# A two-layer block on one core: the rank-8 condition weights are generated between the steps of the first recurrence

## The reference, cut to what matters

```python
# first recurrence (L0_cond2), 512 steps
a = xw_t + prev_h @ Wh                     # xW = x @ Wx + b, 4*256 columns
i, f, o = sigmoid(a[:, :H]), sigmoid(a[:, H:2*H]), sigmoid(a[:, 2*H:3*H])
g = tanh(a[:, 3*H:])
next_c = f * prev_c + i * g;  next_h = o * tanh(next_c)
...
# condition of layer 1 (L1_cond), RANK = 8, D = 256, 8 rows of ada_emb
c = (ada_emb - mu) / sqrt(var + 1e-5) * ln_gamma + ln_beta
h = gelu(c @ W1 + bias1)
w = h @ W2 + bias2                         # W2: 256 x 4*256*8
a1, b1, a2, b2 = [t.reshape(B, D, R) for t in split(w, 4)]
u = x @ a2;  mid = gelu(x @ base_down + u @ b2.T)
out = mid @ base_up.T + (mid @ b1) @ a1.T;  x + out
```

## Time and profile before

| | us |
|---|---|
| median of 3 runs | 4209.75 |
| the profiled execution | 4171.73 |
| its span, first to last instruction | 4170.0 |
| PE busy (matmul) | 3372.0 (81%) |
| weight loads busy | 2464.0 (59%) |
| DVE busy | 2302.2 (55%) |
| ScalarE busy | 1551.2 (37%) |
| POOL busy | 1201.6 (29%) |
| mean granted clock of TensorE | 0.743 |

### The profile page before, as it was taken

One profiled execution on the slowest core, in us unless ns is written; L12 is line 12 of the kernel. 1 busy time (PEld: TensorE's weight loads), 2 busy tenths in 40 slices (PEclk: granted clock), 3 DMA queues, 4 the chain that ended last, 5 costly groups with the idle time before them and its releaser, 6 DMA issues. The chain is left out here.

```text
span 4170.0 us, 141505 instructions
## 1 busy us (share of the span) xinstructions
PE 3372.0 (81%) x57076; PEld 2464.0 (59%) x57076; DVE 2302.2 (55%) x6841; ACT 1551.2 (37%) x5111; POOL 1201.6 (29%) x1588
## 2 busy tenths in 40 slices
PE   6665638888888888479989399999999998999772
PEld 4443317777777777435563156666666657777562
DVE  4449844444444444368801577778877775555333
ACT  0112213333333333257700355556555553444331
POOL 0001260100000000033300064555555555444442
PEclk9789965555555555589959699999999995555686
DMA  4001000000000000111000100000000001110245
GB/s 118 4 30 35 25 20 3 3 3 3 3 3 3 3 3 3 53 49 26 15 29 0 46 2 2 2 2 2 2 2 2 2 12 52 34 33 30 79 119 165
DMA packets 106990, 106.95 MB, mean 26 GB/s; under 512 B 52669, under 2 KB 94086, under 8 KB 105899
## 3 DMA queue, kind: packets, MB, share of 16 engines
q1 hardware_dynamic: 98714, 78.68, 6.7%
q0 software_dynamic: 7824, 21.46, 1.4%
HBM read 71.10 MB, written 29.00 MB: 24 GB/s over the span
## 5 line engine op out<-in xcount | busy, mean ns | idle before, releaser
L638 PE MATMUL banks<-hp,whp 128*128 128x8 f16 x24576 | 741.1, 168 | 153.9 <-DVE hp L695 153.9
L638 PEld LDWEIGHTS banks<-hp,whp 128*128 128x128 f16 x24576 | 697.0, 104 | 235.1 <-DVE hp L695 234.3
L690 DVE SCALAR_TENSOR_TENSOR carry<-ig 128x16 f32<-128x16 f32 x512 | 93.1, 182 | 426.2 <-ACT ig L661 426.2
L661 ACT ACTIVATE ig<-banks 128x32 f32<-128x32 f32 x512 | 100.9, 197 | 610.0 <-PE banks L638 610.0
L1015 ACT ACTIVATE att_PH<-att_stp 128x1024 f16<-128x1024 f32 (+3 forms) x258 | 183.2, 710 | 374.5 <-PE att_stp L833 374.4
L1642 PE MATMUL rnn_banks<-rnn_hp,rnn_whp 128*128 128x8 f16 x6144 | 285.0, 171 | 30.8 <-ACT rnn_hp L1700 9.9
L1642 PEld LDWEIGHTS rnn_banks<-rnn_hp,rnn_whp 128*128 128x128 f16 x6144 | 251.1, 108 | 97.9 <-ACT rnn_hp L1700 69.4
L616 POOL COPY HT<-hist 128x128 f32 x64 | 21.2, 407 | 986.7 <-DVE hp L700 986.7
L1080 POOL TENSOR_TENSOR att_QK<-att_rot,att_QK 128x512 f16<-128x512 f32 x133 | 173.8, 1307 | 338.5 <-ACT att_QK L1007 338.5
L624 PE MATMUL banks<-xs,wxp 128*128 128x64 f16 x3168 | 264.1, 241 | 0.0
L951 DVE TENSOR_TENSOR att_PL<-att_P,att_PH 128x1024 f16<-128x1024 f32 (+3 forms) x257 | 234.0, 930 | 17.3 <-ACT att_P L1021 16.4
(11 more groups left out here) (555 smaller groups left out, 7831.0 us busy)
## 6 DMA issues: line engine op xcount, KB each, us to landing
exp_xt<-expert_rows_scratch SPq DMA_DIRECT2D x80, 129.0 KB, 2.3
edge_cb<-cols_scratch SPq DMA_DIRECT2D x16, 512.0 KB, 3.7
XT<-expert_found_scratch SPq DMA_DIRECT2D x16, 512.0 KB, 4.9
gen_w<-in_L_cond_W_dram SPq DMA_DIRECT2D x2, 3072.0 KB
mod_xn<-in_x_dram SPq DMA_DIRECT2D x8, 512.0 KB
XT<-in_xT_dram SPq DMA_DIRECT2D x1, 4096.0 KB
out_dram<-exp_ob SPq DMA_DIRECT2D x64, 64.0 KB, 2.2
attw_st<-in_L_attn_w_qkvT_dram SPq DMA_DIRECT2D x6, 512.0 KB
```

Source lines behind the costliest of these rows:

```text
L638: last=nc.tensor.matmul(out, whp[:,wpart,k,col:col+128], hp[:,k,hpart], start=False,stop=True,skip_group_check=True)
```

## The change

`load_lstm_weights` is replaced by `prepare_stage`, which brings the recurrence's weights and all small operands of the condition weights (15 transfers), and runs the layer norm, the hidden product and its Gelu; the hidden vector hT stays in SBUF. In `lstm_stage` SP brings W2 in 8 pieces of 128 x 8 columns, each twice (for the even iteration shifted by four places, for the odd one not), into one buffer, when PE has finished with the last piece. PE makes one product behind the projection in every other step of the second half of each iteration, 8 an iteration, 128 in all; at the 17th step it waits for the piece. Behind the loop stand the additions of the bias, the transposes and the copy. ScalarE makes the high parts of wx and wh instead of DVE, and PE's first projections wait for less. The prefetch in `ffn0_stage` and the first block of `cond1_stage` are gone; the setup of constants on POOL moves into `prepare_stage`.

```diff
-def lstm_stage(nc, XT, HT, wx, wh, bias, h0T, T=T):
+def lstm_stage(nc, XT, HT, wx, wh, bias, h0T, g, W2, ident, T=T):
...
+        @block.sync
+        def _(sp):
+            with loop(nc,sp,NIT) as it:
+                sp.wait_ge(generated,it+1)
+                sp.sem_inc(sp_passed,1)
+                for k in range(2):
+                    piece=W2[k*P:(k+1)*P,:].rearrange("p (a n) -> p a n",n=PIECE)[:,bass.ds((it>>1).with_bounds(min_val=0,max_val=7),1),:].rearrange("p a n -> p (a n)")
+                    sp.dma_start(w2[:,k,bass.ds(RANK//2-(it&1)*(RANK//2),PIECE)],piece).then_inc(w2_in,16)
...
             pe.wait_ge(init,2)
-            pe.wait_ge(wsplit,7)
-            pe.wait_ge(h0split,4)
+            pe.wait_ge(w_hi,1)
+            pe.wait_ge(wsplit,4)
             pe.wait_ge(x_staged,2)
+            pe.sem_inc(generated,1)
+            def generate(it,m):
+                r_,k=divmod(m,2)
+                w=w2[:,k,RANK//2:RANK//2+PIECE].rearrange("p (d r) -> p r d",r=RANK)[:,r_]
+                return nc.tensor.matmul(ps_w[:,bass.ds((it*(RANK//2)+r_)*NB,NB)],w,hT[:,k],start=(k==0),stop=(k==1),skip_group_check=True)
             for half in range(2):
                 for tile in TILES: last=project(0,half,*tile)
             last.then_inc(x_projected,1)
+            pe.wait_ge(w_hi,2)
+            pe.wait_ge(wsplit,5)
+            pe.wait_ge(h0split,4)
...
+                    if s==C: pe.wait_ge(w2_in,it*32+32)
                     pe.wait_ge(hi_ready, it*2*C+s)
...
+                    if st==1 and cs%2==1: last=generate(it,cs//2)
+                    if s==2*C-1: last.then_inc(generated,1)
+            pe.wait_ge(biased,8)
+            for j,q in enumerate((0,3)):
+                for o in range(2): i=nc.tensor.transpose(ps_r[0:BR,j*D+o*P:j*D+(o+1)*P],wT[:,q,o,:],ident[:,:])
+            i.then_inc(rows,1)
         @block.scalar
         def _(act):
+            nc.scalar.activation(wxp[:,0],wx[:,:,:],ACT.Copy).then_inc(w_hi,1)
+            nc.scalar.activation(whp[:,0],wh[:,:,:],ACT.Copy).then_inc(w_hi,1)
...
-            for n,(src,dst) in enumerate(((wx,wxp),(wh,whp))):
-                nc.vector.tensor_copy(dst[:,0],src[:,:,:]).then_inc(wsplit,1)
-                dve.wait_ge(wsplit,2*n+1)
-                nc.vector.tensor_tensor(dst[:,1],src[:,:,:],dst[:,0],ALU.subtract).then_inc(wsplit,1)
+            dve.wait_ge(w_hi,1)
+            nc.vector.tensor_tensor(wxp[:,1],wx[:,:,:],wxp[:,0],ALU.subtract).then_inc(wsplit,1)
...
+            dve.wait_ge(w_hi,2)
+            nc.vector.tensor_tensor(whp[:,1],wh[:,:,:],whp[:,0],ALU.subtract).then_inc(wsplit,1)
...
+            dve.wait_ge(generated,NIT+1)
+            for q in range(4):
+                for k in range(2):
+                    at=(q*2+k)*BR
+                    nc.vector.tensor_tensor(wT[:,q,k,:].rearrange("p (b r) -> p b r",r=RANK),ps_w[:,at:at+BR].rearrange("p (r b) -> p b r",b=NB),b2[:,q,k:k+1,:].broadcast_to([P,NB,RANK]),ALU.add).then_inc(biased,1)
+            dve.wait_ge(rows,1)
+            nc.vector.tensor_copy(wR[:,:,:],ps_r[0:BR,:].rearrange("p (q d) -> p q d",q=2))
...
-                for dst,src in prefetch: sp.dma_start(dst,src).then_inc(prefetched,16)
...
-def load_lstm_weights(nc, wx, wh, bias, Wx, Wh, b):
+def prepare_stage(nc, wx, wh, bias, g, early, ident):
...
+            for n,(to,given) in enumerate(early): sp.dma_start(to,given).then_inc(early_in if n<5 else weights_in,16)
...
+            dve.wait_ge(early_in,80)
+            X_=mybir.AxisListType.X
+            step(nc.vector.tensor_reduce(out=st[:,0:1],in_=c[:,:],axis=X_,op=ALU.add))
...
+            for k in range(2): step(nc.vector.tensor_scalar(cT[:,k],ps_c[:,k*NB:(k+1)*NB],ga[:,k:k+1],be[:,k:k+1],ALU.mult,ALU.add))
+            dve.wait_ge(weights_in,160)
             for w in (wx[:,:,3*NH:4*NH],wh[:,:,3*NH:4*NH],bias[:,3*NH:4*NH]): nc.vector.tensor_scalar(w,w,2.0,None,ALU.mult).then_inc(doubled,1)
             dve.wait_ge(doubled,3)
...
+            for o in range(2):
+                for k in range(2): i=nc.tensor.matmul(ps_h[:,o*NB:(o+1)*NB],w1[:,k,o*P:(o+1)*P],cT[:,k],start=(k==0),stop=(k==1))
+            i.then_inc(hid,1)
```

More of the change, by code:

```diff
@@ L587, in lstm_stage @@
         NIT=T//(2*C); HALF=C//2
+        PIECE=P*RANK; w2=sb("gen_w2",[P,2,PIECE+RANK]); BR=NB*RANK
+        ps_w=ctx.enter_context(nc.psum_tensor("gen_ps_w",[P,512],F32)); ps_r=ctx.enter_context(nc.psum_tensor("gen_ps_r",[P,512],F32))
+        hT,b2,wT,wR=[g[n] for n in ("hT","b2","wT","wR")]
+        w2_in=sem("w2_in"); generated=sem("generated"); sp_passed=sem("sp_passed"); biased=sem("biased"); rows=sem("rows"); w_hi=sem("w_hi")
         block=ctx.enter_context(nc.Block())
@@ L1390, in cond1_stage @@
+        up,down,mask,wT,wR,nw,eps,ones=[g[n] for n in "up,down,mask,wT,wR,nw,eps,ones".split(",")]
         u=sb("u",[BR,T]); v=sb("v",[BR,T]); mid=sb("mid",[P,2,T]); sq=sb("sq",[P,2,2,T]); rs=sb("rs",[P,2,T]); rr=sb("rr",[P,2,T])
@@ new lines, in _ @@
+        @block.gpsimd
+        def _(pool):
+            nc.gpsimd.memset(ones[:,:],1.0).then_inc(const,1)
+            nc.gpsimd.memset(eps[:,:],float(np.finfo(np.float32).eps)).then_inc(const,1)
+            nc.gpsimd.memset(st[:,4:5],1e-5).then_inc(const,1)
+            nc.gpsimd.memset(mask[:,:],1.0).then_inc(const,1)
+            pool.wait_ge(const,4)
+            nc.gpsimd.affine_select(out=mask[:,:],in_=mask[:,:],compare_op=ALU.is_ge,fill=0.0,base=0,pattern=[[-RANK,NB]],channel_multiplier=1).then_inc(const,1)
+            pool.wait_ge(const,5)
+            nc.gpsimd.affine_select(out=mask[:,:],in_=mask[:,:],compare_op=ALU.is_ge,fill=0.0,base=RANK-1,pattern=[[RANK,NB]],channel_multiplier=-1).then_inc(const,1)
+            pool.wait_ge(const,6)
@@ L2023, in _ @@
+            dve.wait_ge(weights_in,160)
             for w in (wx[:,:,3*NH:4*NH],wh[:,:,3*NH:4*NH],bias[:,3*NH:4*NH]): nc.vector.tensor_scalar(w,w,2.0,None,ALU.mult).then_inc(doubled,1)
             dve.wait_ge(doubled,3)
+        @block.scalar
+        def _(act):
+            act.wait_ge(dv,5); act.wait_ge(const,3)
+            nc.scalar.activation(st[:,2:3],st[:,1:2],ACT.Sqrt,scale=1.0/D,bias=st[:,4:5]).then_inc(root,1)
+            act.wait_ge(hid,1)
+            for k in range(2): i=nc.scalar.activation(hT[:,k],ps_h[:,k*NB:(k+1)*NB],ACT.Gelu,bias=b1[:,k:k+1])
+            i.then_inc(gel,1)
+            act.wait_ge(gel,1)
@@ L2025, in build, with _ @@
+        @block.tensor
+        def _(pe):
+            pe.wait_ge(dv,7)
+            for k in range(2): i=nc.tensor.transpose(ps_c[:,k*NB:(k+1)*NB],c[:,k*P:(k+1)*P],ident[0:NB,0:NB])
+            i.then_inc(turned,1)
+            pe.wait_ge(dv,9)
+            for o in range(2):
+                for k in range(2): i=nc.tensor.matmul(ps_h[:,o*NB:(o+1)*NB],w1[:,k,o*P:(o+1)*P],cT[:,k],start=(k==0),stop=(k==1))
+            i.then_inc(hid,1)
 def build(nc, a, out):
@@ L2050, in build @@
[L2050 to L2054 removed]
+        late=ctx.enter_context(ExitStack()); g={}
@@ new lines, in build @@
+        for n,shape in (("up",[P,2,D]),("down",[P,2,D]),("mask",[NB*RANK,NB]),("wT",[P,4,2,NB*RANK]),("wR",[NB*RANK,2,D]),("nw",[P,2]),("eps",[P,1]),("ones",[P,P])): g[n]=late.enter_context(nc.sbuf_tensor("adapt_"+n,shape,F32))
+        soon=late.enter_context(ExitStack())
+        for n,shape in (("c",[NB,D]),("w1",[P,2,D]),("b1",[P,2]),("b2",[P,4,2,RANK]),("gamma",[P,2]),("beta",[P,2]),("hT",[P,2,NB])): g[n]=soon.enter_context(nc.sbuf_tensor("gen_"+n,shape,F32))
+        wx,wh,bias=[soon.enter_context(nc.sbuf_tensor("lstm_"+n,shape,F32)) for n,shape in (("wx",[P,2,4*NH]),("wh",[P,2,4*NH]),("bias",[1,4*NH]))]
@@ new lines, in build @@
+        by_p=lambda x: a[x].rearrange("(k p) n -> p k n",p=P)
+        vector=lambda x: a[x].rearrange("(k p) -> p k",p=P)
+        early=[
+            (g["c"][:,:],a["cond_1024"]),(g["w1"][:,:,:],by_p("L1_cond_W1")),(g["b1"][:,:],vector("L1_cond_bias1")),(g["gamma"][:,:],vector("L1_cond_ln_gamma")),(g["beta"][:,:],vector("L1_cond_ln_beta")),(wx[:,:,:],by_p("L0_cond2_Wx")),(wh[:,:,:],by_p("L0_cond2_Wh")),(bias[:,:],a["L0_cond2_b"].rearrange("(a n) -> a n",a=1)),(g["nw"][:,:],vector("L1_attn_norm_weight")),
+            (g["up"][:,:,:],by_p("L1_cond_base_upT")),(g["down"][:,:,:],by_p("L1_cond_base_down"))]+[(g["b2"][:,q],a["L1_cond_bias2"].rearrange("(q k p r) -> q p k r",q=4,k=2,r=RANK)[q]) for q in range(4)]
@@ L2055, in build @@
+        prepare_stage(nc,wx,wh,bias,g,early,ident)
+        lstm_stage(nc,XT,HT,wx,wh,bias,h0T,g,a["L1_cond_W2"],ident)
+        soon.close()
+        ffn0_stage(nc,XT,HT,*[a["L0_ffn_"+n] for n in ("Wq","bq","Wk","bk","Wv","bv","Wr","br","Wo","bo")],ident,g_dram,i_dram)
+        cond1_stage(nc,XT,HT,g)
         late.close()
```

121 lines of the change are left out of this document (20 added, 101 removed).

## The result

The changed kernel takes 4180.88 us (median of 4 runs, 4171.49 to 4188.12) against 4210.12 us of the kernel before (4 runs, 4207.03 to 4212.69). The ratio is 0.9926 with an interval of 0.9914 to 0.9938: faster by 29 us, where 74 us were forecast. The profiled execution took 4171.49 us (span 4169.7, mean granted clock 0.743), that of before 4171.73 us. The two traces have the same length although the medians differ, so the gain must be read by stage.

What follows compares the result with a forecast made beforehand. Bound: a row of stages with barriers, longest the first recurrence, a closed chain of 2.12 us steps. Terms -80.9 + 6 + 5.6 - 4 + 2.2 - 3.3 = -74.4 us gave 4135 us, range 4113 to 4164.

Steps and rivals of the forecast that it cites:

- (a): Condition stage: making the weights and the barrier behind it go, the main loop takes their place; -80.9 us.
- (f): Head selection: without the prefetch's 6 MB burst, DVE's 3.29 us stall goes; -3.3 us, bounds 0 and -6.
- (b): First recurrence: 128 products placed in PE's 0.44 us gaps waiting for hp, 0.05 us each; +6 us.
- the products do not fit: Rival, recurrence: products overrun PE's gap; 4148 us from 0.15 us each, 4190 us wholly exposed; chance 0.12.
- (c): Preparation in front of the recurrence: 15 transfers make it 13.2 us instead of 7.6; +5.6 us, bounds +3 and +9.
- (d): Start of the recurrence: PE begins sooner, with ScalarE rounding wx and wh; -4 us, between 1.1 and 8.3 gained.
- (e): Behind the recurrence's last step: bias addition, transposes and copy now end the block; +2.2 us, bounds 2 and 4.
- Code loading starves beside the pieces: Rival, recurrence: 1 MB bursts at loop turns hold up code; 53 us (4188 us) to 105 us (4240 us); chance 0.05.
- The clock: Rival, recurrence: clock rises to 1.00, steps take 2.05 us instead of 2.12, giving 4093 us; chance 0.04.

Runs made afterwards that it cites:

- experiment 8: The changed kernel, unedited, measured again on chip 8 beside the kernel before: 4175.22 us, ratio 0.9925.
- experiment 2: Changed kernel with only W2's first piece loaded, once ahead of the loop, the other pieces left out of the products: 4145.16 us, one run.
- experiment 3: Changed kernel without the loop's 128 products, pieces still loaded, ps_w filled once ahead of the loop: 4151.56 us, one run.
- experiment 9: Changed kernel plus a tiny Sigmoid ahead of the loop and 128 empty PE increments behind the adjacency stage's projections: 4108.72 us, ratio 0.9829 to the kernel before.

## Why the prediction was wrong

**(a) and (f), the block and the prefetch: right.** -84.2 us forecast, -83.0 measured. The view has both in one stretch. DVE's stall behind the burst of the prefetch is gone, in the same place of the kernel after (37 us behind the start of the head selection, as before):

```profile
1811.76 1.89 DVE L1294 TENSOR_TENSOR pick_term<-pick_is_head,pick_bt 128x512 f32<-128x512 f32 x3
```

**(b), the products: the step that failed.** It was priced at 0.05 us each, +6 us, under the sentence "What covers the product is only PE's wait for hp". That cover was enough: the price is 0. The rival in which the products do not fit falls with it. But the step counted only the time of the instructions. The other way in which the edit can lengthen this loop, late code, was left to a rival and put at nothing in the sum, because "code fetched one packet ahead covers nearly all of it", and the tables that ScalarE holds stand nowhere. Measured is +47.3 us, in two terms that the sum does not have: PE's stalls at the turn, 35 us in the first step against none, and the table loads, 16 to 19 us in the second. In the place of step (b) the runs put: products 0, code at the turn +35 us here and 0 to +41 us by where it lies, table loads +16 us (9 net of what comes back in the third step).

**(c) and (d), preparation and start: right in the sum.** Forecast +5.6 - 4 = +1.6 us; the first recurrent loads begin 1.5 us later (626.8 for 625.3), of which 0.6 us come from the stage ahead. The preparation went as reckoned, about +6.2 us: its transfers end it, as the row of DVE says. ScalarE's rounding took 1.91 us for 2.0 forecast, but PE's start waited for POOL's staging of x, 7.5 us behind the block's start. PE starts 7.7 us behind it, where it was 12.4: 4.7 us gained for 4, and 5.3 by the first recurrent load, inside the bounds of 1.1 and 8.3.

```profile
612.70 0.43 DVE L2003 TENSOR_SCALAR lstm_wx<-lstm_wx 128x512 f32<-128x512 f32 x1 [5.10 <-DMA gen_b<-in_L_cond_bias_dram]
...
614.61 1.91 ACT L683 ACTIVATE wxp<-lstm_wx 128x2048 f16<-128x2048 f32 x1 [4.62 <-PEq L44]
...
620.81 1.29 POOL L619 TENSOR_TENSOR xs<-xf,xs 128x128 f16<-128x128 f32 x1
...
622.35 0.21 PE L633 MATMUL banks<-ones_rows,bp 128*128 128x64 f16 x1 [12.83 <-POOL xs L619]
```

The preparation's own cost, however, was not only its length: it is also where the table loads come from. The sum had its Gelu down as running beside the transfers, at no cost, and did not ask which table it leaves.

**(e), behind the last step: right,** +2.2 us forecast and measured (from the last recurrent product to the head selection's first instruction it is 5.3 us instead of 3.1). DVE's copy closes it:

```profile
1773.07 0.68 DVE L736 COPY adapt_wR<-gen_ps_r 64x512 f32<-64x512 f32 x1 [1.16 <-PE gen_ps_r L679]
```

**The rivals.** "Code loading starves beside the pieces" had the right engine, the right place and nearly the right size: one stall of 3.29 us in each iteration was reckoned, 2.3 us were found. It had the wrong cause: without the pieces nothing changes, and the packet of code comes before the burst. I gave it 0.05, on the argument above. In the kernel after that argument holds within the body, where no step is longer than before the change, and not at the turn. The Trainium skill (Trainium Kernel Development and Optimization, Key Constraints) says that DMAs issued from the SP, ACT and POOL queues share the 16 DMA engines; it does not name the queue of the code there. Here sharing was no cost, since the recurrence with the pieces and without them agrees within the spread of such runs (1142.9 us in the result and 1145.4 in experiment 8, 1144.9 in experiment 2). The clock did not rise, it was 0.50 throughout, as the forecast had it.

The rest of the sum stands: with the Sigmoid and a good place the kernel gains 69.6 us (4178.36 to 4108.72), where 74.4 were forecast, and 16 us of excess in the first two steps (2.2 + 14.1) are still in it, against 5 before. By my estimate from these numbers it would gain 81 us without them, and the forecast's terms with the products at 0 give 80.4.

## What to carry to other kernels

This edit to a long unrolled loop had two prices besides its instructions: the place of the loop's code, which everything in front of it shifts, and the activation table that ScalarE holds on entering. Look at the first steps behind the turn by themselves, for "issue" ahead of PE and for ACT_TABLE_LOAD in the loop, before an edit to the body is blamed; a small activation from the loop's own table, put in front of it, and some empty instructions in an idle stretch are cheap tests. The time of the loop's own branch, by its source line, tells a stall at the turn apart at once. A comparison of two versions of this loop that ignores the place can be off by 3% of the loop (1107 to 1145 us).

## What was not expected of the hardware

- A packet of the instruction queue (3.44 MB in 210 packets from 700 to 1700 us, 16 KB each; 0.9 to 1.5 us) has landed 1.25 to 1.78 us before PE's first load behind a stall, at all 75 turns looked at (15 each of the kernel after and of experiments 2, 3, 8 and 9). From the packet's start to PE that is 2.2 to 3.1 us.
- PE's branch back takes 0.36 us in the kernel before and with 192 increments, and 3.00 us (median) in the kernel after.
- The same loop took 1107.0 to 1144.6 us by the number of empty instructions ahead of it, and not in one direction: 32 and 64 were worse than none, 96, 128 and 160 better. A stall inside the iteration moved 16 weight loads, with their matmuls, for each 32.
- A table load is 1.28 us. The 32 in the loop took 16 us off the second steps when they went: the 16 ahead of ig lay beside PE's stall, the 16 ahead of keep did not.
- PE takes a float32 product of 128 x 128 weights with 8 columns in 0.5 us between two steps (1040.94 to 1041.45) and resumes without a gap, with an address that depends on the iteration.
- The expert stage, which is the same in all kernels, took 249 to 253 us on two chips and 271 to 274 us on a third, and the second recurrence 485 to 491 and 493 to 495 us.
